# Four gather layers of a graph network: how many of 50 steps the tensor engine picks, padded tables, and split messages in the last layer

## The reference

```
h = x @ W;  out = segment_sum(h[src] * norm, dst) + b            # layer 1: two such convolutions
e1, e2 = (efeat @ W_m)*h[src], (efeat @ W_a)*h[src]              # layer 2: softmax over the edges of a node
msg = einsum(h[src], W_rel[type]) * e;   segment_sum(msg, dst)   # layer 3: 90 relations
msg = einsum((edge_attr @ edge_w + edge_b), x[src])              # layer 4: a 16x16 matrix per edge
x + segment_sum(msg, dst) + x @ root_w + root_b
```

## Time and profile before

| | |
|---|---|
| median of 3 runs | 10341.31 us |
| the profiled execution | 10343.91 us, span 10342.1 us |
| PE busy | 7906.1 us, 76% |
| DVE busy | 7421.7 us, 72% |
| ACT busy | 2862.0 us, 28% |
| POOL busy | 7980.6 us, 77% |
| conv1, first to last gather | 259.6 to 1651.3 us |
| conv2 | 1807.9 to 3068.7 us |
| softmax layer | 3211.3 to 6828 us |
| rel | 7072.8 to 8547 us |
| nn | 8748.7 to 10228.6 us |

### The profile page before, as it was taken

How to read it: one execution, slowest core, us unless ns; L and a number is a source line. 1 busy time by engine, 2 the same in 40 slices (tenths; PEclk the granted TensorE clock), 3 DMA queues, 4 the chain that set the end, 5 groups by cost and what they waited for, 6 DMA issues and landing times.

```text
span 10342.1 us, 126982 instructions
## 1 busy us (share of the span) xinstructions
PE 7906.1 (76%) x34167; PEld 3985.8 (39%) x34167; DVE 7421.7 (72%) x13816; ACT 2862.0 (28%) x12162; POOL 7980.6 (77%) x5375
## 2 busy tenths in 40 slices
PE   0899884999993777777777777737999992988883
PEld 0455442455541333333333333314555551444442
DVE  2556551444444999999999999987888782777774
ACT  0111111000003666666666666631000000000000
POOL 4788885777767888888888888846888884888887
PEclk6999996999996777777777777768999995988886
DMA  1333331222223666666666666664222221333331
GB/s 34 92 100 98 91 89 32 61 65 60 61 52 77 194 194 194 194 194 194 194 194 193 195 194 193 195 191 144 78 78 77 67 69 45 98 84 92 92 91 42
DMA packets 501017, 1210.71 MB, mean 117 GB/s; under 512 B 244714, under 2 KB 281742, under 8 KB 480134
## 3 DMA queue, kind: packets, MB, share of 16 engines
q1 hardware_dynamic: 241732, 983.55, 29.4%
q0 software_dynamic: 223712, 118.77, 9.7%
q10 hardware_dynamic: 35440, 106.85, 3.3%
HBM read 415.09 MB, written 787.23 MB: 116 GB/s over the span
## 4 chain that ended last, share of the span: by engine, by line
POOL 37%; PE 21%; issue 20%; DVE 13%; ACT 5%; DMA 2%; DVEq 1%; SPq 1%; ACTq 0%; POOLq 0%
POOL arena L514 37%; PE PS L877 11%; ACT arena L727 5%; PE PS L1011 3%; PE PS L1012 3%; DVE arena L1526 3%; DVE arena L1522 3%; DVE arena L1566 2%; PE PS L899 2%; DVE arena L1535 1%; DVE arena L1546 1%; DVE arena L1644 1%; DVEq L1514 0%; DMA d_nn<-arena 0%; PE PS L988 0%
## 5 line engine op out<-in xcount | busy, mean ns | idle before, releaser
L877 PE MATMUL PS<-arena,TB 125*128 125x500 bf16 (+1 forms) x17325 | 4098.3, 384 | 139.9 <-DVE arena L1272 138.0
L514 POOL DMA_INDIRECT arena<-d_feat,srci x1650 | 2985.8, 1810 | 587.4 <-issue 487.1
L514 POOL DMA_INDIRECT arena<-d_h,srci x1584 | 2053.9, 1297 | 684.8 <-issue 472.8
L877 PEld LDWEIGHTS PS<-arena,TB 125*128 125x128 bf16 (+1 forms) x17325 | 1568.6, 100 | 2360.1 <-issue 981.0
L727 ACT ACTIVATE arena<-PS,arena 125x32 f32<-125x32 f32 x10560 | 1927.6, 482 | 44.4 <-DMA arena<-d_feat,srci 44.4
L1283 DVE SCALAR_TENSOR_TENSOR arena<-arena,lane,PS 128x500 f32<-128x500 f16 x825 | 598.2, 725 | 1526.8 <-PE PS L877 1156.7
L514 POOL DMA_INDIRECT arena<-d_nn,srci x858 | 1217.1, 1418 | 353.6 <-issue 261.1
L514 POOL DMA_INDIRECT arena<-d_rel,irel x858 | 1212.8, 1414 | 307.2 <-issue 261.4
L1272 DVE TENSOR_SCALAR arena<-arena,lane 125x1500 bf16<-125x1500 f16 (+1 forms) x1848 | 1180.4, 697 | 198.7 <-PE PS L877 132.3
L1011 PE MATMUL PS<-arena,ident 125*125 125x512 f32 x1650 | 1090.6, 749 | 207.8 <-DVE arena L1526 206.5
L1566 DVE SCALAR_TENSOR_TENSOR arena<-arena 125x512 f32<-125x512 f32 x1485 | 1107.6, 746 | 0.3
(11 more groups left out here) (261 smaller groups left out, 6052.1 us busy)
## 6 DMA issues: line engine op xcount, KB each, us to landing
d_soft_den<-arena SPq DMA_DIRECT2D x330, 560.0 KB
d_soft_num<-arena SPq DMA_DIRECT2D x330, 560.0 KB
d_soft_max<-arena SPq DMA_DIRECT2D x165, 1120.0 KB
arena<-d_pick SPq DMA_DIRECT2D x99, 750.0 KB
arena<-d_lane SPq DMA_DIRECT2D x99, 750.0 KB
d_x<-arena ACTq DMA_DIRECT2D x165, 241.7 KB
arena<-d_x SPq DMA_DIRECT2D x165, 241.7 KB
d_rel<-arena SPq DMA_DIRECT2D x50, 669.4 KB
```

Source lines behind the costliest of these rows:

```text
L514: gp.indirect_dma_start(out=dst, out_offset=None, in_=table, in_offset=bass.IndirectOffsetOnAxis(ap=index, axis=0)).then_inc(S(sem), 16)
L877: ins = pe.matmul(PS[0:w, 2048 + (q % 3) * 512:2048 + (q % 3) * 512 + QW], TB[:, part, g * LANES * F:g * LANES * F + w], OH[L][i][:, g, at ...
```

## The change

The picks become 26, 28, 24 and 27 of 50 steps for conv1, conv2, rel and nn. conv1 and nn get a seventh quarter, in chunks of 4 and 3, that is narrower: two steps (250 columns) in conv1, three (375) in nn. POOL gathers 24, 22, 26 and 23 steps. `TB` is padded with zeros to 7 x 128 columns, so that all 21 matmuls are 128 wide, in the order 0 to 6. In conv1 `split_tr` moves one quarter later, and ACT's first `x6_out` goes behind `put`. In nn there are nine products in three banks instead of eight in four; `messages` becomes `picked_messages` (before the block's first product) and `pooled_messages` (in front of mask 4), and the scans are in two halves behind masks 4 and 5. Addresses in the arena follow.

```diff
-CHUNKS = {"conv1": (3, 3), "conv2": (4, 3), "rel": (3, 3), "nn": (3, 3)}
+CHUNKS = {"conv1": (4, 3), "conv2": (4, 3), "rel": (3, 3), "nn": (4, 3)}
-XP = {L: Q4 * n for L, n in NQ.items()}
+XP = {"conv1": 26, "conv2": 28, "rel": 24, "nn": 27}
+def picked_cols(L, q):
+    return P * min(Q4, XP[L] - Q4 * q)
+def chunk_cols(L, i):
+    return sum(picked_cols(L, q) for q in range(sum(CHUNKS[L][:i]), sum(CHUNKS[L][:i + 1])))
...
-        TB = sb("TB", [P, PARTS, J * F], bf16)
+        TB = sb("TB", [P, PARTS, NG * LANES * F], bf16)
...
 (ACT, conv1)
-                    if last and x6:
-                        x6_out(*last, 0)
...
-                        for g in (1, 2, 3, 4):
+                        for g in range(5):
                             x6_out(*last, g)
 (PE, pick)
-                for n, g in enumerate((0, NG - 1, *range(1, NG - 1))):
-                    w = min(LANES, J - g * LANES) * F
+                w = picked_cols(L, q)
+                for g in range(NG):
                     for part in range(PARTS):
-                        ins = pe.matmul(PS[0:w, ... + QW],
-                                        TB[:, part, g * LANES * F:g * LANES * F + w], OH[L][i][:, g, at:at + QW],
+                        ins = pe.matmul(PS[:, ... + w],
+                                        TB[:, part, g * LANES * F:(g + 1) * LANES * F], OH[L][i][:, g, at:at + w],
 (PE, sum_lanes)
-                        if t % TRI == 0 and (u >= 4 or not start):
-                            pe.wait_ge(S("n_pr"), NPAIR * NBL + NTRI * b + u - 3)
-                        at = (u % 4) * 512 + (t % TRI) * PW
+                        if t % TRI == 0 and (u >= 3 or not start):
+                            pe.wait_ge(S("n_pr"), NPAIR * NBL + NTRI * b + u - 2)
+                        at = (u % 3) * 512 + (t % TRI) * PW
 (PE, conv1)
-                        if L == "conv1" and last and q < 5:
-                            split_tr(*last, q)
+                        if L == "conv1" and last and 1 <= q < 6:
+                            split_tr(*last, q - 1)
 (DVE)
+            link(v.memset(TB[:, :, J * F:], 0.0))
...
-                def messages(b, s, k):
+                def picked_messages(b, s):
+                    dve.wait_ge(S("n_pr"), NPAIR * NBL + NTRI * (b + 1))
+                    v.tensor_reduce(MN[:, NP[L]:BL, :], TM..., X, ALU.add).then_inc(S("n_dve"), 1)
+                def pooled_messages(b, s, k):
                     n, own = NP[L], S("n_dve")
-                    dve.wait_ge(S("n_pr"), NPAIR * NBL + NTRI * (b + 1))
-                    v.tensor_reduce(MN[:, n:BL, :], TM..., X, ALU.add)
                     dve.wait_ge(S(f"n_g{s}"), upto(L, f"g{s}", 16 * n * (k + 1)))
...
 (DVE, step; last = the block before)
                     mask(b, s, 0, not last)
                     if L == "nn" and last:
-                        product(last[0], last[1], 4)
+                        product(last[0], last[1], 6)
                     one_hot(b, s, k, 1, 0, 4)
+                    if L == "nn" and last:
+                        product(last[0], last[1], 7)
                     mask(b, s, 1, not last)
+                    one_hot(b, s, k, 1, 4, NG)
                     if L == "nn" and last:
-                        product(last[0], last[1], 5)
-                    one_hot(b, s, k, 1, 4, NG)
+                        product(last[0], last[1], 8)
                     mask(b, s, 2, not last)
-                    if L == "nn" and last:
-                        product(last[0], last[1], 6)
-                        product(last[0], last[1], 7)
-                        messages(*last[0:3])
+                    if L == "nn":
+                        if last:
+                            picked_messages(last[0], last[1])
+                            dve.wait_ge(S("n_dve"), 12 * NBL + 3 * last[0] + 1)
+                        product(b, s, 0)
                     if not final:
                         one_hot(b + 1, 1 - s, k + s, 0, 0, 4)
                     mask(b, s, 3, not last)
                     if L == "nn":
-                        product(b, s, 0)
+                        product(b, s, 1)
                     if not final:
                         one_hot(b + 1, 1 - s, k + s, 0, 4, NG)
-                    if last:
+                    if L == "nn" and last:
+                        pooled_messages(*last[0:3])
+                    if L != "nn" and last:
                         scans(*last, 0, 4)
                     for q in range(4, nq):
                         mask(b, s, q, not last)
                         if L == "nn":
-                            for u in ((1,), (2, 3))[q - 4]:
+                            for u in ((2, 3), (4,), (5,))[q - 4]:
                                 product(b, s, u)
-                        if last and q == 4:
+                            if last and q < 6:
+                                scans(*last, 8 * (q - 4), 8 * (q - 3))
+                        elif last and q == 4:
                             scans(*last, 4, F)
```

More of the change, by code:

```diff
@@ L35 @@
 ROW = 3 * CH
-AR = 35200
+AR = 36288
 KX = 6 * F + 3
@@ L188, in graph_layers @@
         SC2 = V[:, BL * F:BL * TW]
-        TM = ar(8988, XP["nn"] * PW)
-        MN = ar(12444, BL * F).rearrange("p (t c) -> p t c", t=BL)
-        E9 = ar(13244, 2 * BL * K9).rearrange("p (s t k) -> p s t k", s=2, k=K9)
+        TM = ar(8124, XP["nn"] * PW)
+        MN = ar(12012, BL * F).rearrange("p (t c) -> p t c", t=BL)
+        E9 = ar(12812, 2 * BL * K9).rearrange("p (s t k) -> p s t k", s=2, k=K9)
         OH = {"conv1": one_hots("conv1", (7250, 16000)), "conv2": one_hots("conv2", (7250, 16000)),
-              "rel": one_hots("rel", (9520, 14770)), "nn": one_hots("nn", (14144, 27200))}
+              "rel": one_hots("rel", (9520, 14770)), "nn": one_hots("nn", (13712, 26400))}
         PI = {"conv1": codes("conv1", (27200, 28950)), "conv2": codes("conv2", (27200, 28950)),
-              "rel": codes("rel", (20020, 25600)), "nn": codes("nn", (19394, 20894))}
+              "rel": codes("rel", (20020, 25600)), "nn": codes("nn", (20712, 31216))}
         LI = {"conv1": codes("conv1", (30700, 32450)), "conv2": codes("conv2", (30700, 32450)),
-              "rel": codes("rel", (27100, 28600)), "nn": codes("nn", (24000, 32450))}
-        MK = {"conv1": masks(1600), "conv2": masks(1600), "rel": masks(3440), "nn": masks(7488)}
+              "rel": codes("rel", (27100, 28600)), "nn": codes("nn", (32904, 34592))}
+        MK = {"conv1": masks(1600), "conv2": masks(1600), "rel": masks(3440), "nn": masks(6624)}
         o = 0
@@ L873, in pick @@
                     pe.wait_ge(S("n_mk"), upto(L, "mk", nq * (b - 1) + nq - 2 + (q - nq) % 3))
-                for n, g in enumerate((0, NG - 1, *range(1, NG - 1))):
-                    w = min(LANES, J - g * LANES) * F
+                w = picked_cols(L, q)
+                for g in range(NG):
                     for part in range(PARTS):
-                        ins = pe.matmul(PS[0:w, 2048 + (q % 3) * 512:2048 + (q % 3) * 512 + QW],
-                                        TB[:, part, g * LANES * F:g * LANES * F + w], OH[L][i][:, g, at:at + QW],
-                                        start=n == 0 and part == 0, stop=n == NG - 1 and part == PARTS - 1)
+                        ins = pe.matmul(PS[:, 2048 + (q % 3) * 512:2048 + (q % 3) * 512 + w],
+                                        TB[:, part, g * LANES * F:(g + 1) * LANES * F], OH[L][i][:, g, at:at + w],
+                                        start=g == 0 and part == 0, stop=g == NG - 1 and part == PARTS - 1)
                 ins.then_inc(S("n_acc"), 1)
@@ L888, in sum_lanes @@
                 pe.wait_ge(S("n_mk"), upto(L, "mk", NQ[L] * b + q + 1))
-                for t in range(q * Q4, q * Q4 + Q4):
+                for t in range(q * Q4, min(q * Q4 + Q4, XP[L])):
                     lanes = MK[L][:, q % 3, t % Q4 * P:(t % Q4 + 1) * P]
@@ L1269, in one_hot @@
                         dve.wait_ge(S("n_acc"), upto(L, "acc", nq * (b - 1) + sum(CHUNKS[L][:i + 1])))
-                    at, n = sum(CHUNKS[L][:i]) * QW, CHUNKS[L][i] * QW
+                    at, n = sum(CHUNKS[L][:i]) * QW, chunk_cols(L, i)
                     for c in range(lo, hi):
-                        ins = v.tensor_scalar(OH[L][i][:, c, :], PI[L][s][0:P, at:at + n], lane[0:P, c:c + 1], None, ALU.is_equal)
+                        ins = v.tensor_scalar(OH[L][i][:, c, 0:n], PI[L][s][0:P, at:at + n], lane[0:P, c:c + 1], None, ALU.is_equal)
                     if hi == NG:
@@ L1470, in picked @@
                 if L == "nn":
-                    for u in range(4, NTRI):
+                    for u in range(6, NTRI):
                         product(NBL - 1, 0, u)
-                    messages(NBL - 1, 0, HALF)
+                    picked_messages(NBL - 1, 0)
+                    pooled_messages(NBL - 1, 0, HALF)
                 scans(NBL - 1, 0, HALF, False, 0, w)
```

30 lines of the change are left out of this document (16 added, 14 removed).

## The result

The changed kernel takes 10215.0 us (median of 4 runs, 10202.3 to 10219.7), the kernel before 10342.5 beside it (4 runs, 10339.2 to 10347.9): ratio 0.9874, interval 0.9857 to 0.9891. The forecast was 10223. The profiled execution of the changed kernel, 10202.3 with a span of 10200.5, was the fastest of its four, so the two profiles are 141.6 us apart and the medians 127.4.

A forecast was written before the change was run, and what follows sets the result against it. POOL was taken to bound conv1, rel and nn, PE conv2; afterwards a PE-DVE ring would hold nn. Terms -43 - 90 + 0 + 15 = -118 on the profiled 10343.9 gave 10226, as median 10223; range 10185 to 10265 (62%).

The forecast's parts named there:

- Padding and conv2: All matmuls 128 wide save 0.187 us a quarter; conv2, at PE's pace, goes from 38.1 to 36.8 a step: -43 us.
- conv1: Stage at POOL's pace: two gathers less per block, 38.9 us instead of 41.8, PE's `split_edges` wait goes: -90 us.
- + 2.4: In conv1, 2.4 us a block that gathers take beyond their undisturbed time beside DVE work, kept unchanged after the change.
- rel: Stage stays at POOL's pace with its gathers unchanged: 0 us (-10 to +5).
- the ring: In nn, DVE's mask 0 waits for PE's lane sum, PE's lane sum for product 2: 45.4 us a step, stage +15.
- 0.5 for handing over: In nn, 0.5 us a step added to the DVE and PE work, making 43.3 us before the clock's share.
- DVE's leg: In nn, DVE's work from mask 0 to product 2: masks, products, one-hots, reduces and 0.3 of waits, 27.7 us.
- 2.1 for the clock: In nn, 2.1 us a step for PE's slow stretch at half clock behind its wait (bounds 0 and 3.2).
- A proper: Rival: nn is not held by the ring, POOL decides, -150 instead of +15, total 10058; 7%.
- B: Rival: half clock fills PE's part of the ring, nn step 49.8 us, stage +155, total 10363; 6%.
- C: Rival: padding gives nothing, the order of groups causes the gaps; conv2 0, nn 18 worse, total 10284; 6%.
- D: Rival: narrow quarters cost as much as full ones in conv1 and nn, +10 + 35, total 10268; 7%.

The follow-up runs named there:

- pad_only_old_order: The kernel before with only the table padded so all matmuls are 128 wide, its old order of groups kept: 10296.5 us against 10348.2, ratio 0.9948.
- conv1_24: The changed kernel with conv1 alone back to 24 picked steps: 10295.3 us against 10348.2 for the kernel before, ratio 0.9949.
- conv1_split_light: The changed kernel with both two-operand subtractions of `split_edges` in conv1 left out: 10162.0 us against 10330.7 for the kernel before.
- conv1_27: The changed kernel with 27 picked steps in conv1, one gather less: 10201.9 us against 10350.0 for the kernel before.
- nn_fill: The changed kernel with 22 unused matmuls put ahead of PE's wait for product 2 in nn: 10197.8 us against 10348.2 for the kernel before.
- nn_bank_fill: The changed kernel with 22 filling matmuls before PE's wait and a fourth PSUM bank for nn's seventh quarter: 10169.4 us, 181 less than the kernel before.
- nn_bank_late: The changed kernel with a fourth PSUM bank for nn's seventh quarter and `pooled_messages` behind products 2 and 3: 10056.8 us against 10350.0, ratio 0.9714.

## Why the prediction came out as it did

*Padding and conv2: right.* 0.187 us a quarter were forecast and 0.22 came (5.21 for 5.43); the step is 36.7 for 36.8, the stage -48 for -43. pad_only_old_order shows that the shape is the cause.

*conv1: mechanism right, one term mis-sized.* Two gathers less are worth 88 us (conv1_24 against the changed kernel; the forecast had 90), PE's wait for `split_edges` fell from 3.4 to 0.2 us a block and POOL rests only for its issue. The failed term is the one held constant, "+ 2.4" for what DVE does to the gathers. It rose to 3.0: from 2.33 to 3.03 by the gathers of all blocks, 0.7 x 33 = 23 us, about what is missing. conv1_24 has 3.07 too, and is 17 us slower than before, so the number of picks is not the cause. The table under conv1_split_light shows what rose: more gathers begin in the second subtraction, 30 in the changed kernel and 33 in conv1_24 instead of 17, and those in the scans are held for longer, though conv1_24 has the same DVE instructions in conv1 as before. So it is the phase between the two engines. conv1_27 shows the other side: there a single gather meets the subtraction, and the excess is 1.74. What moved the phase in the changed kernel is open. The moved transposes, ACT's order and the new order of groups are all in conv1_24; pad_only_old_order, with the padding alone, is at 2.53 and 6 us slower.

*rel: right.* -0.4 us. PE rests more, POOL doesn't notice.

*nn: the ring right, its price 1.0 us a step too high.* Cut the step at PE's lane sum that waits for product 2: DVE's leg runs from mask 0 to it, PE's leg from it to the next mask 0 (means of 20 late steps, us; in the forecast's row 0.5 for handing over is in the step only):

| | DVE's leg | PE's leg | step |
|---|---|---|---|
| forecast | 27.7 | 15.1 + 2.1 for the clock | 45.4 |
| changed kernel | 27.1 | 17.3 | 44.4 |
| nn_fill | 27.6 | 16.4 | 44.0 |
| nn_bank_fill | 27.35 | 15.5 | 42.85 |

What was mis-sized is DVE's leg, 0.6 us shorter than its sum, and the 0.5 for handing over, which the measured legs already hold. PE's leg is as forecast, 17.3 for 17.2. The forecast named both waits and their lengths (6 us for the product; measured 5.8) and overlooked a third, the bank of pick 0 behind the scans. At full clock this wait takes back about half of what the clock gives: 0.9 us on PE's leg in nn_fill, 1.8 with the bank free. What is left of the 0.9 in the whole step is 0.4, because DVE's one-hots took 0.5 longer in nn_fill. With 1.0 us a step less than forecast, 32 steps make 33 us, and +15 becomes -18; measured -11.5. The 6.5 between are not taken apart. Of the 150 us that three gathers less could bring, the rings left 11.5.

*The sum.* Two misses of opposite sign nearly cancel: the forecast had conv1 19 us too short and nn 26 too long (in the profiled execution), with -5 in conv2, -3.5 in the softmax layer and -6.6 elsewhere beside them. That the total came within 8 us of the forecast is in part luck. Of the rivals, A proper (POOL decides in nn) isn't what happened; nn_bank_late shows what it would have brought. It is 293 us faster than before on its own chip, and A's 10058 stands for 283. Two errors hide in that closeness too: its nn gained 168 instead of 150, its conv1 63 instead of 90. B, C and D don't hold; from the start of the narrow quarter to the next instruction it is 3.34 us with 375 columns at full clock (nn_fill; 3.3 forecast).

## What to carry to other kernels

Before taking work off the engine that decides, list the waits by which the others hold one another, through every buffer that turns with q modulo n: where the number of turns is no longer a multiple of n, the edges move. Break all rings at once: compared with the changed kernel's nn stage (1488.2 us) the late messages alone made it 52 us longer, and with the bank they made it 156 shorter. An engine's slow stretch behind a wait is to be priced against the work that runs beside it, not at its own length: 1.8 us on PE's leg here, of which 0.9 counted.

## What the hardware showed that I hadn't expected

DVE's products and subtractions, which read two operands from SBUF, hold POOL's gathers, rows of scans hold some of them, and a reduce none: in nn a gather begun in L1341 takes 3.86 us, and the one begun 1.35 us into the reduce of the same length (L1344, 9235.51 to 9239.11) takes 1.21, in the changed kernel. Of 255 gathers there that began in one of the long reduces of rel and nn none took over 1.3 us. One-hots, with one such operand, hold them too, for less: those of 1250 columns by 0.3 us.
```profile
9232.70 3.86 POOL L524 DMA_INDIRECT arena<-d_nn,srci  x1 [0.30 <-issue]
9236.86 1.21 POOL L524 DMA_INDIRECT arena<-d_nn,srci  x1 [0.30 <-issue]
```
The Trainium skill (SBUF — State Buffer, "Who interferes with whom") says that on this chip a reduce never contends with GpSimd, and the trace agrees. It also says that an instruction with two SBUF inputs contends with a GpSimd instruction that reads SBUF, and a gather reads its row numbers (`srci`) there; but it infers that `tensor_tensor` spares descriptor generation, and here the measurement, 3.86 for 1.21 us, decides against that.

How much they cost depends on where the two engines meet, not only on how long DVE works: 1.7 (conv1_27) to 3.1 us a block (conv1_24) for the same split.

The half clock came behind waits of 5.80 and 7.20 us, in which PE stood idle. Pick 6 behind the first took 4.99 us instead of 3.51, and filling that wait shortened the step by 0.4 us; pick 0 behind the second took 7.41 instead of 4.59.
